# Three-layer graph network on one core: one arc per node and source class by one-hot products instead of a gather

## What is computed

```python
def layer(h, src, dst, Mw, Mb, Uw, Ub, ...):
    msg = concatenate([h[src], h[dst]]) @ Mw.T + Mb
    deg, s1, s2 = segment_sum(1, dst), segment_sum(msg, dst), segment_sum(msg * msg, dst)
    mx, mn = segment_max(msg, dst), segment_min(msg, dst)
    mean = s1 / deg; var = relu(s2 / deg - mean * mean); std = sqrt(var + 1e-30)
    agg = concatenate([mx, mn, std, var])
    u = concatenate([h, agg, agg * logd / 4, agg * 4 / logd]) @ Uw.T + Ub   # logd = log(deg + 1)
    u = batchnorm(u / sqrt(N)); out = leaky_relu(u @ mix_w.T + mix_b) + h
# per layer: h = elu(layernorm(layer(h))); at the end x = layernorm(x + h)
```

## Time and profile before

| | us |
|---|---|
| runs shown | 2145.09 to 2157.81, median 2156.35 of 3 |
| the profiled execution, first to last instruction | 2141.7 |
| stage A, layer 0, 1, 2, by GpSimd's gathers | 110.80 to 708.5; 784 to 1379; 1450 to 2029 |

### The profile page before, as it was taken

One profiled execution on the slowest core, in us unless ns is written; L12 is line 12 of the kernel. 1 busy time (PEld: TensorE's weight loads), 2 busy tenths in 40 slices (PEclk: granted clock), 3 DMA queues, 4 the chain that ended last, 5 costly groups with the idle time before them and its releaser, 6 DMA issues. The chain is left out here.

```text
span 2141.7 us, 10446 instructions
## 1 busy us (share of the span) xinstructions
PE 682.6 (32%) x2156; PEld 402.8 (19%) x2156; DVE 1096.6 (51%) x2178; ACT 455.6 (21%) x1024; POOL 1235.7 (58%) x1358
## 2 busy tenths in 40 slices
PE   5611233132322470323132232362113322233265
PEld 5311121011111230112111111131101211112122
DVE  8600755464644843445464463572525664466464
ACT  0103321122111154111111111136101221112125
POOL 7673666676666127745675675406756666576504
PEclk9975666565655685566565666686556666656677
DMA  4363333333333033323332232204323333333200
GB/s 59 105 167 113 93 103 103 91 99 92 92 91 91 18 112 113 111 66 99 96 101 76 88 103 75 65 27 145 106 84 101 93 88 93 88 103 96 76 0 30
DMA packets 97107, 190.18 MB, mean 89 GB/s; under 512 B 30792, under 2 KB 56984, under 8 KB 97040
## 3 DMA queue, kind: packets, MB, share of 16 engines
q0 software_dynamic: 59968, 160.78, 26.6%
q1 hardware_dynamic: 37077, 28.77, 4.9%
HBM read 168.75 MB, written 17.75 MB: 87 GB/s over the span
## 5 line engine op out<-in xcount | busy, mean ns | idle before, releaser
L742 POOL DMA_INDIRECT G<-p_by_rank,index x774 | 734.8, 949 | 560.2 <-issue 227.8
L742 POOL DMA_INDIRECT G<-p_by_node,index x387 | 367.4, 949 | 225.0 <-issue 120.3
L921 PE MATMUL ps<-wide_ident,agg 128*128 128x128 f32 x288 | 80.3, 434 | 1209.3 <-issue 701.2
L1470 DVE TENSOR_TENSOR ps<-ps,G 128x1024 f32<-128x1024 f32 (+3 forms) x222 | 250.3, 1127 | 191.2 <-issue 78.4
L921 PEld LDWEIGHTS ps<-wide_ident,agg 128*128 128x128 f32 x288 | 51.5, 217 | 1239.5 <-issue 721.9
L936 PE MATMUL ps<-w_u_sb,aggT 128*128 128x384 f32 x576 | 284.3, 654 | 0.0
L1714 DVE SCALAR_TENSOR_TENSOR var<-tot,rdeg,msq 128x128 f32<-128x128 f32 x75 | 26.1, 348 | 426.4 <-ACT msq L1109 407.8
L936 PEld LDWEIGHTS ps<-w_u_sb,aggT 128*128 128x128 f32 x576 | 162.6, 282 | 144.7 <-issue 119.1
L1135 ACT ACTIVATE u_sb<-ps 128x128 f32<-128x128 f32 x75 | 20.7, 277 | 721.1 <-remote 509.0
L1472 DVE TENSOR_TENSOR ps<-ps,G 128x512 f32<-128x512 f32 (+3 forms) x222 | 141.6, 638 | 0.0
L1471 DVE TENSOR_TENSOR ps<-ps,G 128x512 f32<-128x512 f32 (+3 forms) x222 | 141.5, 637 | 0.0
(11 more groups left out here) (280 smaller groups left out, 1328.3 us busy)
## 6 DMA issues: line engine op xcount, KB each, us to landing
G<-p_by_rank,index POOLq DMA_INDIRECT x774
p_by_rank<-base SPq DMA_DIRECT2D x18, 512.0 KB
G<-p_by_node,index POOLq DMA_INDIRECT x387
p_by_node<-G SPq DMA_DIRECT2D x6, 514.0 KB
w_u_sb<-in_w_u SPq DMA_DIRECT2D x3, 768.0 KB
x_r<-rows_by_rank SPq DMA_DIRECT2D x1, 1600.0 KB
G<-shared_rows SPq DMA_DIRECT2D x12, 53.0 KB
windows<-src_pad SPq DMA_DIRECT2D x1, 624.8 KB, 14.1
```

The lines of the kernel that those rows point to most:

```text
L742: g.indirect_dma_start(G[:, n % R, j, 0:w], None, table, bass.IndirectOffsetOnAxis(ap=named, axis=0))\
L921: ins = nc.tensor.transpose(ps[:, 2, i * D:(i + 1) * D], agg[:, t % 2, i * D:(i + 1) * D], ident[:, :])
L1470: TT(run[:, 0:nk, :], run[:, 0:nk, :], G[:, n % R, 0:nk, 0:2 * D], ALU.add)
```

## The change

Source nodes are numbered by node, and a class is 128 consecutive nodes. For the first six classes (B = 6) each target node has its best arc from that class (one at most) taken out of its list. What is left goes through the gathers as before, with fewer slots: 318 own slots and 9 joint gathers in 97 groups. The taken arc arrives by TensorE: a class's 128 rows lie in SBUF (class_rows), SP broadcasts the taken rows' numbers of two tiles to all partitions (picked_rows, 128 x 1536), VectorE compares them with the partition number (hots_of_pair), and TensorE's product of that one-hot and the class gives for each target its row, zero where there is none for the sums (L995, into bank 7) and a very low number for the extremes (L1002, into bank 5). VectorE folds the latter into the base at once (fold), and the sums after six classes. To use one operation for both ends, LOW is held negated, as a maximum. There are 13 pairs of tiles (PAIRS) and 78 such batches per layer, each at a group of the list (BATCH_AT), with TensorE's part one batch ahead (PICK_AT). In layers 1 and 2 GpSimd gathers the six class blocks by rank.

Setup gains, on VectorE, take (finds class, row and key of each arc, and the best per class) before the sorting, which now goes by arcs left, and close_up (closes the gaps in the lists) before the rows are written. The ring has R = 11 groups. x_r lies in base, and SP loads x a second time at the end. The order of turn, update, turn_update, and of combine and statistics, is now the same for all tiles to FAR.

```diff
-    KW = PLAN[T - 1]
+    B = 6
+    PLAN, BEYOND, KW = slot_plan(N, E, T, B)
+    KX = PLAN[T - 1]
+    KW = max(KW, KX + B)
...
-    R = 14
+    R = 11
...
+    PAIRS = [(t, min(2, T - t)) for t in range(0, T, 2)]
+    BATCH_AT, reached = [], len(AHEAD)
+    for c, (t, _) in enumerate(PAIRS):
+        due = tile_groups[t][0 if t == T - 1 else 1] - 1
+        if c == 1:
+            reached = END_OF[0] + 2
+        BATCH_AT += [reached + (k + 1) * (due - reached) // B for k in range(B)]
+        reached = due
+    PICK_AT = [len(AHEAD)] + BATCH_AT[:-1]
...
+            def pick(l, k):
+                c, s = divmod(k, B)
+                t, nt = PAIRS[c]
...
+                if s == 0:
+                    pe.wait_ge(hot_ready.sem, hot_ready.at(l, c + 1))
+                    if c:
+                        pe.wait_ge(pick_summed.sem, pick_summed.at(l, c))
+                hots = [hot[:, c % 2, (i * B + s) * P:(i * B + s + 1) * P] for i in range(nt)]
+                for i in range(nt):
+                    mm(picked_sums[:, 2 * i * D:2 * (i + 1) * D], hots[i], classes[:, s, 0:2 * D],
+                       start=s == 0 and i == 0, stop=s == B - 1 and i == nt - 1)
+                if k == B:
+                    pe.wait_ge(borrowed.sem, borrowed.at(l, 1))
+                elif k:
+                    pe.wait_ge(pick_folded.sem, pick_folded.at(l, k))
+                for i in range(nt):
+                    ins = mm(picks[:, 2 * i * D:2 * (i + 1) * D], hots[i], classes[:, s, 2 * D:4 * D],
+                             start=True, stop=True)
+                ins.then_inc(pick_ready.sem, 1)
...
+            def fold(l, k):
+                c, s = divmod(k, B)
+                t, nt = PAIRS[c]
+                dve.wait_ge(pick_ready.sem, pick_ready.at(l, k + 1))
...
+                ends = base[:, t:t + nt, TOP:LOW + 1:2, :]
+                TT(ends, ends, picks[:, 0:2 * nt * D].rearrange("p (t a d) -> p t a d", a=2, d=D), ALU.max)\
+                    .then_inc(pick_folded.sem, 1)
+                if s == B - 1:
...
+                    TT(sums, sums, picked_sums[:, 0:2 * nt * D].rearrange("p (t a d) -> p t a d", a=2, d=D), ALU.add)\
+                        .then_inc(pick_summed.sem, 1)
...
-                    if n in END and END[n] <= FAR:
-                        if END[n] >= 2:
-                            combine(l, END[n] - 2)
-                        if END[n] >= 3:
-                            statistics(l, END[n] - 3)
...
+                    if n - 3 in END and END[n - 3] <= FAR:
+                        combine(l, END[n - 3])
+                    if n - 5 in END and END[n - 5] <= FAR:
+                        statistics(l, END[n - 5])
...
+                    for k, at_group in enumerate(BATCH_AT):
+                        if at_group == n:
+                            fold(l, k)
+                            if k % B == B // 2 and 1 <= k // B < len(PAIRS) - 1:
+                                hots_of_pair(l, k // B + 1)
```

In take, per batch of tiles, for each class a masked key and its maximum, then for each class a comparison and an addition:

```diff
+                for s in range(B):
+                    ch.step(STT(spare[s % 2], of, float(s), into, ALU.is_equal, ALU.mult))
+                    ch.wait()
+                    ch.step(v.tensor_reduce(best[:, s, t0:t1], spare[s % 2], AX.X, ALU.max))
...
+                for s in range(B):
+                    ch.step(TT(spare[s % 2], into, per_node(best[:, s, :], t0, t1, KC), ALU.is_equal))
+                    ch.wait()
+                    ch.step(TT(out, out, spare[s % 2], ALU.add))
```

More of the change, by code:

```diff
@@ L46, in restart, with poisson, convolve, nodes_over @@
             self.n = 0
-def slot_plan(n_nodes, n_edges, n_tiles):
-    mean = (n_edges - n_nodes) / n_nodes
[L54 to L58, removed]
+def poisson(mean, n):
+    law = [math.exp(-mean)]
+    for k in range(1, n):
+        law.append(law[-1] * mean / k)
+    return law
+def convolve(a, b, n):
+    return [sum(a[i] * b[k - i] for i in range(k + 1)) for k in range(n)]
+def nodes_over(law, n_nodes):
+    tail, beyond = 1.0, []
+    for p in law:
+        tail -= p
+        beyond.append(n_nodes * max(tail, 0.0))
+    return beyond
+def slot_plan(n_nodes, n_edges, n_tiles, classes):
+    mean = (n_edges - n_nodes) / n_nodes
+    n = 4 * int(mean) + 64
+    window = next(k for k, b in enumerate(nodes_over(poisson(mean, n), n_nodes)) if b <= 0.05)
+    of_class = mean * (P - 1) / n_nodes
+    one = poisson(of_class, n)
+    left = [one[0] + one[1]] + one[2:] + [0.0]
+    law = poisson(mean - classes * of_class, n)
+    for _ in range(classes):
+        law = convolve(law, left, n)
+    beyond = nodes_over(law, n_nodes)
     plan = []
@@ L146, in build @@
     AT = range(T - 11, T - 3)
-    WIDE = range(T - 7, T - 3)
-    assert all(PLAN_T[t] - 1 >= (18 if t in WIDE else 16) for t in AT)
+    SORTED = min(PLAN_T[t] for t in AT) - 1
     for a in (0, 1, 2, 3):
@@ L187, in build @@
     END = {tile_groups[t][-1]: t for t in range(T)}
+    END_OF = [tile_groups[t][-1] for t in range(T)]
     CLOSE = {tile_groups[t][-1]: t for t in range(T - 1)}
@@ new lines, in _ @@
+            ch.step(TS(small[:, 1, :], deg[:, :], -1.0, None, ALU.add))
+            dve.wait_ge(s_const, 5)
+            for b in range(len(BATCHES)):
+                shift_windows(b)
+                take(b)
+            ch.wait()
+            ch.step(STT(key_b[:, :], arcs_nat[:, :], float(BINS - 2), real[:, :], ALU.min, ALU.add))
+            ch.step(v.tensor_copy(best_i[:, :, :], best[:, :, :]))
+            ch.wait()
+            TT(hot_bin[:, :, :], digits[:, 0:BINS, :],
+               key_b[:, :].rearrange("p (a t) -> p a t", a=1).to_broadcast([P, BINS, T]),
+               ALU.is_equal).then_inc(s_bins, 1)
@@ L1516, in order_slots @@
[L1516 to L1523 removed]
+                A, spare = sort_a, sort_b
@@ new lines, in order_slots @@
+                named = index[:, AT[0]:AT[-1] + 1, 0:SORTED]
+                ch.step(v.tensor_copy(A[:, :, :], named))
+                ch.wait()
+                for first in range(2):
+                    w = SORTED - first
+                    while w > 1:
+                        h = w // 2
+                        one, two = A[:, :, first:first + h], A[:, :, first + w - h:first + w]
+                        ch.step(TT(spare[:, :, 0:h], one, two, ALU.max))
+                        ch.step(TT(two, one, two, ALU.min))
+                        ch.wait()
+                        ch.step(v.tensor_copy(one, spare[:, :, 0:h]))
+                        ch.wait()
+                        w -= h
@@ L1628, in extras @@
                 xc = Chain(dve, s_xch)
-                valid, pos, new = ex_f[:, 0:1], ex_f[:, 1:2], ex_f[:, 2:3]
+                valid, pos, new, word_no, near = (ex_f[:, i:i + 1] for i in range(5))
                 def of_tile(ap, t):
```

472 lines of the change are left out of this document (305 added, 167 removed).

## The result

The changed kernel takes 2320.34 us (median of 4 runs, 2315.98 to 2326.83), the one before 2156.28: ratio 1.0797, 95% interval 1.0751 to 1.0843. It is 8% slower; 2330 was forecast. The total is right, its make-up only in part, as the experiments show.

A forecast was written before the change was run, and what follows sets the result against it. GpSimd's gather issue, then TensorE's number of records, was taken to bound a stage. 2141.7 + 78 (setup) + 99 (stages, fewer gathers and pick pauses together) + 14.7 (runs above profile) = 2333, said as 2330 us; 8-in-10 range 1980 to 2690.

The forecast's parts named there:

- Setup: VectorE's picking of arcs and closing of gaps before the first gather: +78 us, bounds 60 and 95.
- Fewer gathers: GpSimd in stage A: 198 gathers fewer at 1.25 us, -248 us if GpSimd sets the end.
- The comparison: VectorE's 13 one-hot comparisons per layer, 1.8 us each, might stretch gather issues by 0 to 70 us; taken as 0.
- Picks: Stage A: 1200 more TensorE records per layer, held while GpSimd gathers; stages of 619 to 626 us, +99 us net.
- 64c + 0.8 x (416 - 14c) = 1968 - 64, c = 30: Stage A: c rounds of 64 records at speed, others at 0.8 per us; 30 pauses of 7 us, 626 us.
- The other signs: Signs per layer or stage: VectorE waits over 200 us for picks, TensorE's busy time is near 350 us.
- a stock of 64: Stage A: some 64 TensorE records go at full speed, again after each long pause, before about one per gather.
- The forecast's own range: Total of 2200 to 2560 us, from pauses of 4 to 10 us and a setup of 60 to 95.
- Turnaround: Between layers: GpSimd's 75 us of turnaround stays as it is.
- rival C: Short ring: four stalls a layer each cost 15 us more with 11 groups; 2166 us, no change; chance 0.06.
- the 15 us that were added for the runs above the profiled execution: Whole kernel: median of runs, 2156.35 us, is 14.7 above the profiled span of 2141.7; added back to the sum.
- rival A: Stage A: picks are free since TensorE has room, GpSimd's gather count decides; 1986 us, 8% faster; chance 0.25.

The follow-up runs named there:

- e8: Kernel before with 30 unread bf16 products added after each update of tiles 1 to 21; 2279.7 us, ratio 1.063.
- e3: Kernel before with 15 unread fp32 products 128x256 added after each update of tiles 1 to 21; 2293.1 us, ratio 1.066.
- e2: Changed kernel with one slot more for the last tile, products for the sums left out for four of six classes; 2313.4 us, ratio 1.077.
- e7: e6 with the products for the sums left out for four of six classes, all waits kept; 2099.3 us, ratio 0.978.
- e6: Changed kernel with one slot more for the last tile and its shared slots reaching one place further, so no list runs over; 2104.9 us, ratio 0.981.
- e4: Kernel before with a ring of 11 groups instead of 14, all else the same; 2127.2 us, ratio 0.993.
- e11: e6 with a ring of 6 groups instead of 11; 2077.7 us, ratio 0.965.

## Why the prediction was right, and where it was not

**Setup: right.** 78 forecast, 73.0 measured, by the step it was reckoned with (60 instructions a batch more, in VectorE's unbroken row up to the last list, which ends 77 us later).

**Fewer gathers: right.** 954 own ones for 1161, still one per 1.25 us (mean 963 ns busy and 0.30 between, against 949 before). The 14 ns more are 13 us over all of them. The comparison (0 taken, up to 70 bounded) takes 1.03 us, not 1.8, and has little part in it: of the gathers over 1.05 us only 5 stand mainly beside one, 2 us in excess; more stand beside VectorE's additions from the ring.

**Picks: the mechanism half right, the size too large.** The step was "64c + 0.8 x (416 - 14c) = 1968 - 64, c = 30", with 7 us a pause: 210 us of pauses per layer. Measured are 161, 149 and 152 us in 37, 33 and 33 pauses: the count near, the size 4.5 instead of 7. (The other signs in layer 1: VectorE waits 162 us for picks, not over 200, and TensorE is busy for 316 us, not 350.) That TensorE is held while GpSimd gathers back to back, at about one record per gather, is shown by the rows of e8 and e3. That a stock of 64 comes first, so that the stage follows from the number of records, is refuted by the 150 records in e8 and by e2 and e7. The forecast's own range has a wrong sum besides: 30 pauses of 4 to 10 us and a setup of 60 to 95 give some 2050 to 2620 by its own terms, not 2200 to 2560.

In e6 one run of 22 gathers looks like this. TensorE's instructions in the 22 us up to 1235 and the 9 after them, then the timeline of GpSimd, TensorE and VectorE:

```profile
1213.00:1235.00 22.00, 15.62 (x55) 10.34 (x53) 13.03 (x27) 3.92 (x8) 16.56 (x18) 0.84 0.38 115
1235.00:1244.00 9.00, 0.20 (x1) 0.00 (x0) 0.00 (x0) 0.28 (x1) 4.31 (x5) 0.66 0.30 86
```

```profile
1213.25 0.95 POOL L855 DMA_INDIRECT G<-p_by_rank,index  x1 [4.58 <-DVE ps L1696]
...
1233.31 1.03 PE L1003 MATMUL ps<-class_rows,picked_hots 128*128 128x256 f32 x4
...
1234.18 1.03 PE L996 MATMUL ps<-class_rows,picked_hots 128*128 128x256 f32 x4
...
1239.58 0.95 POOL L855 DMA_INDIRECT G<-p_by_rank,index  x1 [0.30 <-issue]
...
1244.37 0.69 DVE L1860 TENSOR_TENSOR base<-base,ps 128x512 f32<-128x512 f32 x1 [14.60 <-issue]
...
1245.11 2.08 PE L1003 MATMUL ps<-class_rows,picked_hots 128*128 128x256 f32 x4 [9.90 <-DVE base L1860]
...
1248.59 0.95 POOL L855 DMA_INDIRECT G<-p_by_rank,index  x1 [8.06 <-DVE ps L1696]
```

Over a hundred records go at full speed in the 22 us up to 1235 (55 matmul and 53 weight-load records), then one in 9 us. Here it is the result that is late: the pick recorded at 1233.31 is folded at 1244.37, and TensorE's next pick (1245.11) waits for that fold. GpSimd fills its ring until 1240.5, VectorE has its pick 4 us after that and GpSimd its place 4 us later. So it is with most long waits, not with all: of e6's 17 waits of VectorE for a pick over 7 us 15 end after GpSimd has stopped, twelve of them 3.0 to 4.0 us after, and two (at 881.81 and 1522 us) end while it gathers on, as does VectorE's wait until 156.41 in the earlier trace rows.

My reading is that a stall mostly ends by GpSimd's stop and not by the number of records that are open, so that taking a third of the products away changes little, while products that stand ahead of every awaited one, as in e3 and e8, bring more stalls (GpSimd's pauses in layer 1 over 0.6 us: 12 and 13 against 9, and 144 and 138 us against 99). It fits the runs, but no run stops GpSimd on purpose to test it. What decides when the hold sets in (13 gathers after the start in layer 0 of before, about 17 in e6) is open, and so is what holds TensorE.

**Turnaround: missed.** I had it "stays"; it fell by 15 and 13 us, since the ring is shorter (the table; e4 has 15 and 7). The end fell by 16, of which e4's ring of 11 gives 4; where the rest comes from isn't shown. Costing R = 11 at nothing, or as rival C had it at +15 us per stall, was wrong in sign.

**The loop for left-over arcs: missed altogether.** No term and no rival named it. The new plan is drawn from a convolution of laws and sized for each shared slot to the mean and two deviations of the nodes that reach it, and for the fullest node to 0.05 nodes expected beyond. It costs 215 us (e6 against after), more than the whole slow-down of 164 us. It looks like an unlucky draw, but the kernel gives another reason: the law takes a node's picks out of its whole list, while take looks for them in the first 24 arcs only (KC = 24). Counted over the whole lists, the same drawn arcs leave 31 at place 127 and 25 at place 119, and no list runs over. This is counted from the inputs; no run has it.

So the sum is: setup +73, gathers -248, pauses +175 (462 against 287 in all three layers), the loop +222 (what stage A holds beyond 1.25 us a gather and its pauses), turnarounds and end -44, together +178 against 183 of the spans. The forecast's 2330 came out by luck: two misses, +222 (the loop) and -44, met a term that was 168 too large (630 of pauses against 462); the 15 us that were added for the runs above the profiled execution weren't there either (the profiled one is the slowest of the four). The claim "slower" was right for this kernel and this draw; its reason, that held TensorE results eat the gain, was not: with the same products and no overflow the kernel is 2% faster (1% at an equal ring), where rival A, picks free, would have been 1986, or some 1940 with the shorter turnarounds. Of those the picks eat about 160 us, by this subtraction, half of what I gave them.

## What to carry to other kernels

A fallback path for rare data must be read as part of the change: when a plan is cut closer, check that the plan's law counts what the code does, check on the actual data whether the path is entered, and what entering costs (here 69 to 74 us a layer for one or two arcs, most of it a loop over 25 tiles of which 24 have nothing). An engine that is idle by its busy rows may still be late: ask what its results do while GpSimd issues DMAs back to back, and read it off a row of instructions that wait for nothing. A change that also alters the ring's length needs the old kernel with the new length beside it: e6 gains 40 us on before, but only 22 on e4. And a ring that lets the producer run far ahead has a price at the end of a stage, where the consumer has to work the ring off before the next stage can start; e11, with 6 groups and no overflow, is the fastest complete kernel of the study (2077.7 us, 3.5% below before).

## What was not expected of the hardware

TensorE's independent instructions come 2.1 to 2.8 us apart, each 0.3 to 0.4 us long and with nothing to wait for that the trace names, while GpSimd issues a 128-row gather every 1.25 us; after GpSimd's stop 45 records go in 11 us (e8).

The Trainium skill ("SBUF — State Buffer", section "SBUF: two separate sides") says of the engines' side of SBUF that TensorE never waits on anyone. For reads of SBUF no run here contradicts that, but its instructions were held by something that goes along with the gathers, for bf16 (e8) and fp32 (e3) alike. What it is stays open.

A turn of VectorE's loop with value loads, a branch and one 0.15 us copy takes 2.40 us in layer 1 and 2.24 us in layers 0 and 2 of the changed kernel.
